# First attention of an eight-layer kernel as a pipeline over sequences, and other slots in its scan

## The chip, the cores and the metric

The kernel runs on one core of a Trainium2 chip. The metric is the device time of one execution in microseconds (us), the median of three runs. The core has five engines with their own in-order queues: TensorE (PE: products and transposes, results in eight PSUM banks), VectorE (DVE), ScalarE (ACT), GpSimd (POOL) and SyncE (SP, which issues DMAs). They meet through semaphores only. All data is float32 unless said otherwise.

## The reference

Eight layers in a row over x of 8 sequences x 512 tokens x 128. Each takes the layer norm of x and adds its answer to x: cosine attention, top-2 experts, feature attention, switch experts, a selective scan, expert-choice experts, attention with relative positions, threshold experts. The change concerns the first layer, the norm and router of the second, and the scan. Cut to these:

```
n = layernorm(x)
Q, K, V = n @ Wq.T + bq, n @ Wk.T + bk, n @ Wv.T + bv          # 128 each
Q = Q / max(norm(Q), 1e-12);  K = K / max(norm(K), 1e-12)
out = softmax(Q @ K.T) @ V                                     # one head, 512 x 512 per sequence
h = relu(out @ W1.T + b1);  h = relu(h @ W2.T + b2)            # 128, 512
x = x + h @ W3.T + b3

n = layernorm(x)
logits = n @ router_w                                          # 8 experts, two are taken per token
...
# selective scan: n -> conv, silu -> xc; (dt, B, C) = projections of xc; 16 states per channel
h[t] = h[t-1] * exp(dt[t] * A) + dt[t] * B[t] * xc[t];   y[t] = sum over states of h[t] * C[t]
y = (y + xc * D) * silu(z);  x = x + y @ W_out
```

## The kernel before

x stays in SBUF as 32 tiles of 128 tokens x 128 (`chip.x`), four tiles a sequence. Every layer is one or more blocks; at the end of a block all engines meet at a barrier (`end_layer` L133, and the end of each `nc.Block`).

`load_stage` (L162) loads x in two transfers of 1 MB, the identity and some tables, turns the relative-position table into a line and waits for all of it. `cosine_attention` (L208) then loads its weights on SP, and the weights of later layers behind them; at L159 SP issues 16 broadcasts of 0.5 MB for the fourth layer (`prepare_later_layers`). Its loop runs twice with four sequences (`W = 4`) per turn. In a turn all four sequences go through one step, then all four through the next; every engine's queue has the steps in this order:

1. VectorE: statistics (L144, L148); ScalarE: square root (L346); VectorE: reciprocal and normalise (L296, L298).
2. TensorE turns the rows (L389), ScalarE copies them out of PSUM (L349), TensorE projects to q, k, v (L396, 384 columns), VectorE adds the bias (L305).
3. Lengths: ScalarE squares (L356), VectorE sums (L310), ScalarE root (L359), VectorE inverts and scales (L313 to L316). TensorE turns q and k (L402), ScalarE copies (L363).
4. Scores (L410), exponential on ScalarE (L367), weighing of v with a column of ones for the denominator (L418), VectorE copies and divides (L324 to L329).
5. Turn o (L425), first layer (L430), second (L435), third (L443); ScalarE does copies and relu (L370 to L377), VectorE adds the bias and then adds to x (L334, L338).

GpSimd prepares tiles for later layers here (`held.prepare`, `features.prepare`) and else does nothing. The function `Banks` (L50) gives each result its PSUM bank by a written list, and with it the waits: a bank is filled only once the last result in it was read.

`top2_glu_experts` (L1044) begins with `normalise_and_route` (L464), a block of its own: statistics and inverse on VectorE and ScalarE, normalise on GpSimd (L532), turned on TensorE (L579), copied (L552), multiplied with the router (L559), with filler products between (`keep_running`, L567); SP stores the normalised rows to memory, from where the experts fetch them. `route` (L596) follows with a copy of the logits out of PSUM (L647) and the softmax and top two on VectorE.

`selective_scan` (L2598) has 128 steps m, 16 states n for each of 8 sequences q. Every engine's queue is written out over m, and what belongs to the next sequences stands in numbered slots n. Per step: SP brings a row of B to all partitions (L2676); GpSimd multiplies it with du (`dBu`, L2731); ScalarE makes the decay in PSUM (`decay`, L2873, two steps ahead); VectorE runs the recurrence (`recur`, L2974, 128x1024) and weighs the state with C (`weigh`, L2983); TensorE spreads C over the partitions (`spread`, L3079, into one bank) and adds up the weighed states (`add_up`, L3096). For states 0, 3 and 6 GpSimd weighs (L2686, from a copy of C by ScalarE, L2779), and `ADDED_AT` says in which slot TensorE adds these. Per sequence TensorE also has `through` (L3086), the step sizes (`step_sizes`, L3067, two halves in one bank), transposes (`turn`, L3037), convolution (L3046), gate (L3053), projection (L3060) and output (`give_out`, L3105). VectorE's `gains(k)` (L2960 to L2967) makes from mean and deviation the factors for normalised rows; `gains(2)` stands right before the first recurrence and serves 24 tiles. ScalarE's `rows_of(q)` (L2759) and `keep_normed(q)` (L2786) use them. `late` is 2 for sequence 0 and 0 for the others.

## Time and profile before

| | |
|---|---|
| median of 3 runs | 3111.35 us (3110.55 to 3114.8) |
| profiled execution | 3111.72 us, its span 3110.0 us |
| mean granted TensorE clock | 0.954 of full |
| TensorE busy | 2814.7 us (91% of the span) |
| VectorE, ScalarE, GpSimd busy | 1643.1, 1511.5, 1591.5 us (53%, 49%, 51%) |
| load stage | 0 to 13.8 us |
| first attention | 13.8 to 212.6 us |
| norm and router of the second layer | 213.7 to 236 us |
| scan | 869 to 1357 us |

The busy time of an engine says how much it had to do, not what set the end; that is read stage by stage from the windows and from the idle time ahead of an instruction (the last bracket of a timeline's row, with the one that ended it). TensorE's clock is given as a share of 2.4 GHz; a window of 0.5 is 1.2 GHz. A float32 product shows as two records, a transpose as one.

### The profile page before, as it was taken

The numbers are of one execution on the slowest core, as the hardware profiler recorded it, in microseconds if no ns is written. First come the engines' busy times: TensorE is split into PE (matmuls) and PEld (weight loads), VectorE is DVE, ScalarE is ACT, GpSimd is POOL, SyncE is SP. The second block draws the span as 40 slices with busy tenths as digits, with TensorE's granted clock in tenths as the row PEclk, the third lists the DMA queues.
The fourth block names the chain that finished last, engine by engine and source line by source line (L and its number), as shares of the span: only waits on it lengthen the run. The fifth ranks groups of instructions, "written<-read, shape, count | busy, mean of one in ns | idle before, by whom it ended". The sixth has DMA issues, their size and how long they took to land. (4 is left out here: it accounts for less than half of the span.)

```text
span 3110.0 us, 44512 instructions
## 1 busy us (share of the span) xinstructions
PE 2814.7 (91%) x14327; PEld 1760.4 (57%) x14354; DVE 1643.1 (53%) x4042; ACT 1511.5 (49%) x3086; POOL 1591.5 (51%) x1622
## 2 busy tenths in 40 slices
PE   6796997896778899767989999999999999999999
PEld 4564996775733344337974444444444444777776
DVE  4436444755368999974335555555555555211112
ACT  3431332332667877622235666666666664433333
POOL 0011775423768999933434555555555554699100
PEclk9898998887999999988989999999999999999999
DMA  5001667101122222243000000000000000000000
GB/s 174 0 24 56 206 206 188 43 1 40 49 82 70 79 75 82 74 122 116 22 12 1 1 0 0 0 0 0 0 0 0 0 1 13 16 8 8 14 7 28
DMA packets 91000, 141.36 MB, mean 45 GB/s; under 512 B 12315, under 2 KB 48038, under 8 KB 90838
## 3 DMA queue, kind: packets, MB, share of 16 engines
q1 hardware_dynamic: 76502, 116.83, 12.1%
q0 software_dynamic: 9728, 19.94, 2.6%
q10 hardware_dynamic: 4608, 2.56, 0.3%
q8 instruction: 86, 1.41, 0.2%
q14 instruction: 76, 0.62, 0.1%
HBM read 122.71 MB, written 24.97 MB: 47 GB/s over the span
## 5 line engine op out<-in xcount | busy, mean ns | idle before, releaser
L1790 POOL TENSOR_TENSOR l3a_p<-l3a_p,l3a_rden 128x512 f32<-128x512 f32 x512 | 521.5, 1040 | 482.2 <-DVE l3a_rden L1826 479.5
L1816 DVE CUSTOM_DVE_ANT_0 l3a_p<-bank,relative_bias 128x512 f32<-128x512 f32 x512 | 333.4, 689 | 211.2 <-PE bank L1965 204.4
L1886 ACT ACTIVATE l3a_p<-l3a_p,l3a_low 128x512 f32<-128x512 f32 x512 | 365.4, 719 | 4.5 <-DVE l3a_low L1816 4.5
L1974 PEld LDWEIGHTS bank<-ident,l3a_p 128*128 128x128 f32 x2048 | 228.5, 141 | 162.5 <-issue 157.9
L2731 POOL TENSOR_TENSOR l2a_dBu<-l2a_du,l2a_bs 128x1024 f32<-128x1024 f32 x128 | 299.1, 2351 | 32.9 <-DVE l2a_h L2974 30.6
L1892 ACT COPY l3a_pT<-bank 128x512 f32<-128x512 f32 x256 | 150.2, 587 | 324.2 <-PE bank L1974 323.8
L2974 DVE TENSOR_TENSOR_SCAN l2a_h<-bank,l2a_dBu 128x1024 f32<-128x1024 f32 x128 | 290.5, 2280 | 9.5 <-ACT bank L2873 8.3
L1559 ACT ACTIVATE l3f_h<-bank,l3f_b 128x512 f32<-128x512 f32 x256 | 175.5, 687 | 244.4 <-PE bank L1667 241.1
L1965 PE MATMUL bank<-l3a_kT,l3a_qT 64*128 64x512 f32 x1024 | 291.3, 645 | 1.2 <-ACT l3a_kT L1877 0.7
L1974 PE MATMUL bank<-ident,l3a_p 128*128 128x128 f32 x2048 | 273.6, 277 | 0.6 <-ACT l3a_pT L1892 0.5
L1676 PEld LDWEIGHTS bank<-l3f_w,l3f_h 128*128 128x128 f32 x2048 | 237.7, 192 | 27.2 <-issue 27.2
L1625 DVE SCALAR_TENSOR_TENSOR x<-bank,l3f_gates,x 128x128 f32<-128x128 f32 x256 | 72.1, 344 | 338.6 <-PE bank L1676 338.4
L1676 PE MATMUL bank<-l3f_w,l3f_h 128*128 128x128 f32 x2048 | 237.9, 275 | 0.0
L1983 PE MATMUL bank<-l3a_pT,l3a_v 128*64 128x512 f32 x1024 | 233.9, 599 | 0.0
L1667 PE MATMUL bank<-l3f_xnT,l3f_w 128*128 128x512 f32 x512 | 232.6, 599 | 0.8 <-ACT l3f_xnT L1550 0.8
L1822 DVE COPY l3a_pT<-bank 128x512 f32<-128x512 f32 x256 | 174.4, 681 | 54.5 <-PE bank L1974 54.3
L3096 PE MATMUL bank<-l2a_hc,ident 128*128 128x512 f32 x416 | 201.4, 608 | 1.9 <-DVE l2a_hc L2983 1.1
L2873 ACT ACTIVATE bank<-l2a_dt,scan_a_neg 128x511 f32<-128x511 f32 x256 | 165.1, 680 | 59.3 <-DVE l2a_h L2974 56.0
L1965 PEld LDWEIGHTS bank<-l3a_kT,l3a_qT 64*128 64x128 f32 x1024 | 78.5, 186 | 161.9 <-issue 157.2
L1019 PE MATMUL bank<-l0fe_xT,l0fe_wi 128*128 128x256 f32 x640 | 147.7, 385 | 1.7 <-issue 1.1
L1667 PEld LDWEIGHTS bank<-l3f_xnT,l3f_w 128*128 128x128 f32 x512 | 93.7, 193 | 95.7 <-issue 95.7
L966 ACT ACTIVATE l0fe_g<-bank,l0fe_wi 128x256 f32<-128x256 f32 x160 | 67.0, 470 | 158.9 <-PE bank L1019 156.0
(523 smaller groups left out, 5008.0 us busy)
## 6 DMA issues: line engine op xcount, KB each, us to landing
l2a_bs<-l2a_b_rows SPq DMA_DIRECT2D x128, 256.0 KB, 3.3
l0fe_wi<-in_L_ffn_in_dram SPq DMA_DIRECT2D x40, 516.0 KB, 4.9
l0fe_wo<-in_L_ffn_out_dram SPq DMA_DIRECT2D x40, 320.0 KB, 3.3
by_place<-by_distance SPq DMA_DIRECT2D x16, 512.0 KB, 14.5
relative_bias<-by_place SPq DMA_DIRECT2D x16, 448.0 KB, 11.5
l3f_w<-in_L_ffn_W_dram SPq DMA_DIRECT2D x16, 256.0 KB, 3.1
switch_out<-in_L_ffn_out_dram SPq DMA_DIRECT2D x1, 2560.0 KB, 19.2
switch_in<-in_L_ffn_in_dram SPq DMA_DIRECT2D x1, 2064.0 KB, 14.4
```

What stands on the lines that cost most here:

```text
L1559: act.activation(h[q][:, j, :], chip.psum[j][:], ACT.Gelu_apprx_tanh, bias=b1[:, e * J + j:e * J + j + 1]).then_inc(hidden_taken, 1)
L1667: pe.matmul(chip.psum[j][:], w1[e % 2][:, j * P:(j + 1) * P], xnT[:, q * S:(q + 1) * S], start=True, stop=True).then_inc(hidden_summed, 1)
L1676: ins = pe.matmul(y_bank[k % 3][:, t * D:(t + 1) * D], h[q][:, j, t * P:(t + 1) * P], w2[e % 2][:, j, :], start=(j == 0), stop=(j == J - 1))
L1790: ins = pool.tensor_tensor(a, a, rden[:, t, h:h + 1].to_broadcast([P, S]), ALU.mult)
L1816: bk.drain(dve.tensor_tensor_reduce(p[u % 2][h][:, t, :], ps(job)[:], bias[:, u % HP * 2 + h, b0:b0 + S], 1.0, 3.0e38, ALU.add, ALU.min, l ...
L1886: ins = act.activation(a, a, ACT.Exp, bias=low[h][:, t:t + 1], scale=-1.0, accum_out=den[:, t, h:h + 1])
L1965: bk.fill(pe.matmul(ps(job)[:], qT[u % 2][half[h], t * P:(t + 1) * P], kT[u % 2][half[h], :], start=True, stop=True), job)
L1974: ins = pe.transpose(ps(job)[:, t * P:(t + 1) * P], p[u % 2][h][:, t, kt * P:(kt + 1) * P], chip.ident[:])
L1983: ins = pe.matmul(ps("av")[half[h], :], v[u // GP % 2][:, kt, c:c + DK3], pT[h][:, kt, :], start=(kt == 0), stop=(kt == TPS - 1))
L2731: pool.tensor_tensor(dBu[m % ND][:], du[q % 2][:], bcast(bs[m % NB][:], n_before=CH), ALU.mult).then_inc(dBu_ready, 1)
L2974: dve.tensor_tensor_scan(h[m % NH][:].rearrange("p c s -> p (c s)"), dA[m % NA].rearrange("p c s -> p (c s)"), dBu[m % ND][:].rearrange("p ...
L3096: ins = pe.matmul(y_bank[j][:], chip.ident[:], weighed[:, j, :], start=False, stop=(m % N == N - 1))
```

## The change

`load_stage` is gone; its loads and the line for the fourth layer are in the attention's block. x comes in eight transfers, one per sequence, each with a semaphore of its own, on SP; weights are issued by ScalarE's queue. The attention is written out for all eight sequences with no loop: in turn i each engine has scores and weighing of sequence i, the MLP of i-1, the norm and router of i-2 on the way out, and transposes and projection of i+2, in an order given step by step for each engine. Inverse roots are powers of -0.5 on GpSimd (`root`, `invert`), which also normalises both ways, adds b3 to x and prepares the later layers' tiles. Outgoing rows are stored as they come; the logits are copied to SBUF and given to `route`, and `normalise_and_route` isn't called for this layer. In the scan the late gains go to GpSimd behind its third product, and `keep_normed`, `rows_of`, the second half of the step sizes and the addition of state 0 have other slots; TensorE has two fillers more in slot 0 of sequences 1 to 7, and one more at the start. The diff, cut to its core:

```diff
+def cosine_attention(chip, a, w, held, w_scan, features, w_features, xn_rows, logits):
...
+        order = [(("line", c), c) for c in range(2)] + [(("xT", 0), 4), (("xT", 1), 5)]
+        order += [(("qkv", q, t), t) for q in range(AHEAD) for t in range(TPS)] + [(("qT", 0), 6), (("kT", 0), 7)]
+        for i in range(B + 2):
+            now, behind, coming, turning, leaving = i < B, 1 <= i <= B, i + AHEAD < B, i + 1 < B, 2 <= i
+            order += [(("s", i, t), t) for t in range(TPS)] if now else []
+            order += [(("oT", i - 1), 6), (("h1", i - 1), 6)] if behind else []
+            order += [(("xT", i + AHEAD), 7)] + [(("qkv", i + AHEAD, t), 7) for t in range(TPS - 1)] if coming else []
+            order += [(("av", i, t), 4 + t % 2) for t in range(TPS)] if now else []
+            order += [(("h2", i - 1, j), j) for j in range(J)] if behind else []
+            order += [(("qT", i + 1), 6), (("kT", i + 1), 7)] if turning else []
+            order += [(("nT", i - 2), 4)] if leaving else []
+            order += [(("y", i - 1), 6)] if behind else []
+            order += [(("logits", i - 2), 5)] if leaving else []
+            order += [(("qkv", i + AHEAD, TPS - 1), 7)] if coming else []
...
+                sp.dma_start(chip.ident[:], a["ident"]).then_inc(ident_loaded, 16)
+                for q in range(B):
+                    sp.dma_start(chip.x[:, cut(q), :], w["x"][q].rearrange("(t p) d -> p t d", p=P)).then_inc(x_loaded[q], 16)
+                sp.dma_start(chip.before[:], a["before"]).then_inc(kept_loaded, 16)
+                sp.dma_start(chip.count[:], a["count"].partition_broadcast(P)).then_inc(kept_loaded, 16)
+                sp.dma_start(chip.token_no[:], a["token_no"]).then_inc(kept_loaded, 16)
                 held.load(sp, w_scan)
                 features.load(sp, w_features)
+                sp.wait_ge(line_stored, 16)
                 prepare_later_layers(chip, sp)
+                sp.wait_ge(zeros_ready, 1)
+                sp.dma_start(xn_rows[0:1, :], chip.zeros[0:1, 0:D]).then_inc(rows_stored, 16)
+                for q in range(B):
+                    sp.wait_ge(left_ready, q + 1)
+                    rows = xn_rows[1 + q * S:1 + (q + 1) * S, :].rearrange("(t p) d -> p t d", p=P)
+                    sp.dma_start(rows, xn_all[:, cut(q), :]).then_inc(rows_stored, 16)
+                sp.wait_ge(kept_loaded, 48)
+                sp.wait_ge(rows_stored, 16 * (B + 1))
...
+                def root(q, n):
+                    pool.wait_ge(mv_ready[n], q + 1)
+                    chip.apart(pool)
+                    c.link(pool.tensor_scalar(var[n][:, cut(q)], mv[n][:, cut(q), 1], LN_EPS, 0.0, ALU.add, ALU.add))
+                    c.link(pool.tensor_tensor(rstd[n][:, cut(q)], var[n][:, cut(q)], minus_half[:].to_broadcast([P, TPS]), ALU.pow))
+
+                def normalise(q, n, out, ready):
+                    chip.apart(pool)
+                    for t in range(TPS):
+                        at = q * TPS + t
+                        ins = pool.tensor_scalar(out[:, t, :], chip.x[:, at, :], minus_mean[n][:, at:at + 1], rstd[n][:, at:at + 1], ALU.add, ALU.mult)
+                    ins.then_inc(ready, 1)
+
+                def come(q):
+                    root(q, "in")
+                    if q >= 2:
+                        bk.wait_filled(pool, ("xT", q - 2), 0)
+                    normalise(q, "in", xn[q % 2], xn_ready)
+
+                def add_bias(q):
+                    pool.wait_ge(xn_ready, q + 1)
+                    pool.tensor_tensor(chip.x[:, cut(q), :], chip.x[:, cut(q), :], bcast(b3[:], n_before=TPS), ALU.add).then_inc(biased, 1)
+
+                def invert(q):
+                    pool.wait_ge(ss_ready, q + 1)
+                    chip.apart(pool)
+                    c.link(pool.tensor_scalar(low[:, q], ss[:, q], 1e-24, 0.0, ALU.max, ALU.add))
+                    pool.tensor_tensor(inv[:, q].rearrange("p t n -> p (t n)"), low[:, q].rearrange("p t n -> p (t n)"),
+                                       minus_half[:].to_broadcast([P, 2 * TPS]), ALU.pow).then_inc(inv_ready, 1)
+
+                pool.wait_ge(half_ready, 1)
+                come(0)
+                come(1)
+                invert(0)
+                come(2)
+                pool.wait_ge(rest_loaded, 16 * 7)
+                for q in range(3):
+                    add_bias(q)
+                for i in range(B + 2):
+                    if i >= 2:
+                        root(i - 2, "out")
+                    if i + 1 < B:
+                        invert(i + 1)
+                    if i >= 2:
+                        normalise(i - 2, "out", xn_all[:, cut(i - 2), :], left_ready)
+                    if i + 3 < B:
+                        come(i + 3)
+                        add_bias(i + 3)
+                    if i == 2:
+                        held.prepare(chip, pool)
+                    if i == 3:
+                        features.prepare(pool)
...
+                come(0)
+                come(1)
+                for k in range(2):
+                    take_line(k)
+                for k in range(2):
+                    bk.wait_read(dve, ("line", k), 0)
+                dve.sem_inc(lined, 1)
+                come(2)
+                dve.wait_ge(qkv_loaded, 16 * 6)
+                for t in range(TPS):
+                    take_qkv(0, t)
+                sum_squares(0)
+                for t in range(TPS):
+                    take_qkv(1, t)
+                scale(0)
+                for i in range(B + 2):
+                    if i >= 2:
+                        add(i - 2)
+                    if i + 1 < B:
+                        sum_squares(i + 1)
+                    if i + AHEAD < B:
+                        take_qkv(i + AHEAD, 0)
+                    if i + 1 < B:
+                        scale(i + 1)
+                    if i < B:
+                        take_weighed(i, 0)
+                        take_weighed(i, 1)
+                    if i + AHEAD < B:
+                        take_qkv(i + AHEAD, 1)
+                    if i < B:
+                        take_weighed(i, 2)
+                    if i + AHEAD < B:
+                        take_qkv(i + AHEAD, 2)
+                    if i < B:
+                        take_weighed(i, 3)
+                    if i + 3 < B:
+                        come(i + 3)
+                    if i < B:
+                        divide(i)
+                    if i + AHEAD < B:
+                        take_qkv(i + AHEAD, 3)
...
+                for q in range(AHEAD):
+                    take_xT(q)
+                square(0)
+                take(("qT", 0), qT[0][:])
+                take(("kT", 0), kT[0][:])
+                act.wait_ge(rest_loaded, 16 * 7)
+                for i in range(B + 2):
+                    if i < B:
+                        exponential(i, 0)
+                        exponential(i, 1)
+                    if i + 1 < B:
+                        square(i + 1)
+                    if 1 <= i <= B:
+                        take(("oT", i - 1), oT[:])
+                    if i < B:
+                        exponential(i, 2)
+                        exponential(i, 3)
+                    if i + AHEAD < B:
+                        take_xT(i + AHEAD)
+                    if 1 <= i <= B:
+                        take_h1(i - 1)
+                        take_h2(i - 1, 0)
+                        take_h2(i - 1, 1)
+                    if i + 1 < B:
+                        take(("qT", i + 1), qT[(i + 1) % 2][:])
+                    if 1 <= i <= B:
+                        take_h2(i - 1, 2)
+                        take_h2(i - 1, 3)
+                    if i >= 2:
+                        take(("nT", i - 2), nT[i % 2][:])
+                    if i + 1 < B:
+                        take(("kT", i + 1), kT[(i + 1) % 2][:])
+                    if i >= 2:
+                        take_logits(i - 2)
...
+                for i in range(B + 2):
+                    if i < B:
+                        scores(i, 0)
+                        scores(i, 1)
+                    if 1 <= i <= B:
+                        turn_o(i - 1)
+                    if i < B:
+                        scores(i, 2)
+                        scores(i, 3)
+                    if i + AHEAD < B:
+                        turn_x(i + AHEAD)
+                    if 1 <= i <= B:
+                        first(i - 1)
+                    if i + AHEAD < B:
+                        project(i + AHEAD, 0)
+                    if i < B:
+                        weigh(i, 0)
+                    if 1 <= i <= B:
+                        second(i - 1, 0)
+                    if i < B:
+                        weigh(i, 1)
+                    if 1 <= i <= B:
+                        second(i - 1, 1)
+                    if i + AHEAD < B:
+                        project(i + AHEAD, 1)
+                    if i + 1 < B:
+                        turn_q(i + 1)
+                    if i < B:
+                        weigh(i, 2)
+                    if 1 <= i <= B:
+                        second(i - 1, 2)
+                    if i + AHEAD < B:
+                        project(i + AHEAD, 2)
+                    if 1 <= i <= B:
+                        second(i - 1, 3)
+                    if i < B:
+                        weigh(i, 3)
+                    if i >= 2:
+                        turn_out(i - 2)
+                    if i + 1 < B:
+                        turn_k(i + 1)
+                    if 1 <= i <= B:
+                        third(i - 1)
+                    if i >= 2:
+                        route_out(i - 2)
+                    if i + AHEAD < B:
+                        project(i + AHEAD, 3)
...
-        SHARED, LATER, ADDED_AT = (0, 3, 6), 4, {0: 5, 3: 12, 6: 13}
+        SHARED, LATER, ADDED_AT = (0, 3, 6), 4, {0: 6, 3: 12, 6: 13}
...
+                def late_gains():
+                    cut = slice(*PARTS[2])
+                    pool.wait_ge(inverted, 1)
+                    c.link(pool.tensor_tensor(shifts[:, :, cut], inv[:, :, cut], bcast(mv[:, cut, 0], n_before=2), ALU.mult))
+                    chip.apart(pool)
+                    pool.tensor_scalar(shifts[:, :, cut], shifts[:, :, cut], -1.0, 0.0, ALU.mult, ALU.add).then_inc(inv_ready, 1)
+                    pool.tensor_scalar(own_gain[:, cut], inv[:, 0, cut], 1.0, 0.0, ALU.add, ALU.add).then_inc(gains_ready, 1)
...
+                    if m == 2:
+                        late_gains()
...
-                    if m in (10, 15):
-                        keep_normed((10, 15).index(m))
+                    if m in (8, 11):
+                        keep_normed((8, 11).index(m))
...
-                        if n == 2:
+                        if n == 2 + late:
                             rows_of(q + 2)
...
-                gains(2)
+                cut = slice(*PARTS[2])
+                dve.wait_ge(std_ready, 3)
+                dve.reciprocal(inv[:, :, cut], std[:, :, cut]).then_inc(inverted, 1)
...
-                keep_running(5, c_bank)
+                keep_running(6, c_bank)
...
+                    if n == 0 and q:
+                        bk.wait_read(pe, ("bc", q + 1) if q + 1 < B else ("z", q - 1, 1), 0)
+                        keep_running(2, chip.psum[7])
                     if n == 1:
                         through(q)
+                    if n == 3 + late and q + 1 < B:
+                        step_sizes(q + 1, 1)
                     if m in dve_no:
                         add_up(m)
                     if m in pool_adds:
                         add_up(pool_adds[m])
-                    if n in (1 + late, 2 + late) and q + 1 < B:
-                        step_sizes(q + 1, n - 1 - late)
+                    if n == 1 + late and q + 1 < B:
+                        step_sizes(q + 1, 0)
...
-        load_stage(chip, a["L0_attn_x"], a["ident"], a["before"], a["count"], a["token_no"],
-                   a["L3_attn_rel_bias"], a["L3_attn_onehot"])
-        chip.end_layer()
```

## Rows read from the trace of the kernel before

**Rows 1.** Page, part 1: busy us (share of span) xinstructions.

```profile
PE 2814.7 (91%) x14327; PEld 1760.4 (57%) x14354; DVE 1643.1 (53%) x4042; ACT 1511.5 (49%) x3086; POOL 1591.5 (51%) x1622
```

**Rows 2.** Windows: length, busy PE, PEld, DVE, ACT, POOL; clock, DMA share, GB/s.

```profile
0.00:14.00 14.00, 3.59 (x4) 0.41 (x4) 1.75 (x8) 0.00 (x1) 0.19 (x4) 1.00 0.66 181
14.00:50.00 36.00, 18.68 (x74) 13.72 (x75) 29.35 (x91) 13.20 (x23) 6.26 (x10) 0.91 0.82 261
50.00:114.00 64.00, 62.32 (x352) 44.70 (x350) 14.45 (x48) 28.78 (x44) 0.00 (x0) 1.00 0.08 26
114.00:150.00 36.00, 21.39 (x82) 14.71 (x83) 29.18 (x88) 12.86 (x24) 0.00 (x0) 0.76 0.00 0
0.00:237.00 237.00, 187.72 (x970) 131.53 (x970) 101.46 (x363) 90.00 (x152) 20.30 (x46) 0.95 0.22 66
```

**Rows 3.** Timeline of TensorE: start us, us, instruction, count [idle before, releaser].

```profile
24.04 3.67 PE L389 MATMUL bank<-ident,l0a_rows 128*128 128x128 f32 x16 [16.58 <-DMA l0a_b<-in_L_attn_b_dram]
27.51 10.53 PE L396 MATMUL bank<-l0a_w_qkv,l0a_turned 128*128 128x384 f32 x32
44.84 4.46 PE L402 MATMUL bank<-ident,l0a_h 128*128 128x128 f32 x24 [6.80 <-DVE l0a_h L316]
...
50.70 13.90 PE L410 MATMUL bank<-l0a_qT,l0a_kT 128*128 128x512 f32 x32
64.44 14.46 PE L418 MATMUL bank<-l0a_qkv,l0a_E 128*128 128x129 f32 x128
78.73 2.27 PE L425 MATMUL bank<-ident,l0a_rows 128*128 128x128 f32 x16
80.84 3.60 PE L430 MATMUL bank<-l0a_turned,l0a_w 128*128 128x512 f32 x8
```

**Rows 4.** Timeline where the norm stage ends and route begins.

```profile
231.39 1.74 POOL L532 TENSOR_SCALAR l0f_xn_all<-x,l0fr_rstd,l0fr_shift 128x128 f32<-128x128 f32 x4 [0.45 <-DVE l0fr_shift L523]
...
234.08 2.00 PE L559 MATMUL bank<-l0fr_router,l0fr_xnT 128*128 128x8 f32 x16
...
236.52 0.42 DVE L647 COPY l0fg_logits<-bank 128x256 f32<-128x256 f32 x1 [5.34 <-PEq L484]
```

**Rows 5.** GpSimd in later layers: the power by line, an addition by group.

```profile
L1514 POOL TENSOR_TENSOR l3f_rstd<-l3f_var,l3f_minus_half x8: 1028/1028/1031, 2639.4 to 2662.2; 128x4 f32<-128x4 f32 x8
...
L1790 POOL TENSOR_TENSOR l3a_p<-l3a_p,l3a_rden 128x512 f32<-128x512 f32 x512 | 521.5, 1040 | 482.2 <-DVE l3a_rden L1826 479.5
```

**Rows 6.** Window in the steady part of the scan, columns as above.

```profile
1075.00:1130.00 55.00, 50.11 (x131) 21.88 (x134) 52.00 (x33) 43.44 (x67) 51.30 (x24) 0.97 0.27 78
```

**Rows 7.** Groups of VectorE, 906 to 1346: busy us, mean ns | idle before.

```profile
L2983 DVE TENSOR_TENSOR l2a_hc<-l2a_h,bank 128x1024 f32<-128x1024 f32 x102 | 122.3, 1199 | 20.8 <-PE bank L3079 12.1 <-remote 8.7
```

**Rows 8.** Timeline of VectorE in the scan, rows with idle time ahead.

```profile
922.27 2.29 DVE L2974 TENSOR_TENSOR_SCAN l2a_h<-bank,l2a_dBu 128x1024 f32<-128x1024 f32 x1 [2.88 <-ACT bank L2873]
...
965.07 2.29 DVE L2974 TENSOR_TENSOR_SCAN l2a_h<-bank,l2a_dBu 128x1024 f32<-128x1024 f32 x1 [1.46 <-ACT bank L2873]
969.37 2.29 DVE L2974 TENSOR_TENSOR_SCAN l2a_h<-bank,l2a_dBu 128x1024 f32<-128x1024 f32 x1 [2.01 <-ACT bank L2873]
985.38 1.22 DVE L2983 TENSOR_TENSOR l2a_hc<-l2a_h,bank 128x1024 f32<-128x1024 f32 x1 [3.72 <-PE bank L3079]
...
1041.37 1.22 DVE L2983 TENSOR_TENSOR l2a_hc<-l2a_h,bank 128x1024 f32<-128x1024 f32 x1 [2.38 <-remote]
...
1096.07 1.22 DVE L2983 TENSOR_TENSOR l2a_hc<-l2a_h,bank 128x1024 f32<-128x1024 f32 x1 [2.29 <-PE bank L3079]
```

**Rows 9.** Gains by line: duration ns min/median/max, first and last start.

```profile
L2965 DVE SCALAR_TENSOR_TENSOR l2a_shifts<-l2a_mv,l2a_inv x3: 161/376/2145, 876.0 to 901.6; 128x4 f32<-128x4 f32 x2, 128x24 f32<-128x24 f32 x1
...
L2967 DVE TENSOR_SCALAR l2a_own_gain<-l2a_inv x3: 160/163/2319, 876.1 to 903.8; 128x4 f32<-128x4 f32 x2, 128x24 f32<-128x24 f32 x1
```

**Rows 10.** Windows of 2 us at a turn of the scan, columns as above.

```profile
1028.00:1030.00 2.00, 0.00 (x0) 0.00 (x0) 2.00 (x2) 1.71 (x3) 2.00 (x2) 1.00 0.25 55
...
1032.00:1034.00 2.00, 2.00 (x3) 0.67 (x2) 2.00 (x2) 1.38 (x4) 2.00 (x2) 0.50 0.02 7
```

477 lines of the change are left out of this document (227 added, 250 removed).

## The prediction, made before the changed kernel ran

> **What bounds the kernel now.** I read the page's totals first: TensorE is busy 91% of the span [rows 1], so the question is what stands in the missing 9% and what changes hands where. Then the windows by stage, for the first 237 us, all of which the change rewrites [rows 2]. The reader is to see two kinds of stretch. In 50 to 114 us TensorE is busy 62.3 of 64 us. In 0 to 14, 14 to 50 and 114 to 150 us it is busy 3.6, 18.7 and 21.4 us, and there VectorE has 29 of 36 us: four sequences go through each step together, so at the two heads of the loop TensorE stands before the norm, the projection's evictions and the lengths. The row of the whole stretch gives VectorE 101.5 and ScalarE 90.0 us over 8 sequences, 12.7 and 11.3 each; neither can be what paces a stage in which TensorE needs more than that. Third, TensorE's timeline, for the price of each step and the waits before it: idle 16.6 us ahead of the first transposes and 6.8 us ahead of the turned q and k [rows 3]. Last the end of the norm stage [rows 4]: last normalise over at 233.13, route's copy of the logits at 236.52, its first own operation at 236.98.
>
> In the scan VectorE is the pace: 52.0 of 55 us, GpSimd 51.3, TensorE 50.1 [rows 6]. VectorE's idle time in 906 to 1346 us is, above all, 20.8 us ahead of the weighing [rows 7], and the timeline shows where it lies, at the turns from one sequence to the next [rows 8].
>
> The sums are made against the profiled execution: 3111.72 us, of which the span is 3110.0 and 1.7 lie around it. It is 0.4 us above the median of 3111.35, which I neglect.
>
> **First attention: what TensorE has to do.** From rows 3, start to start, per sequence: a transpose 0.132 us (16 in 2.11), 20 of them (x, q, k, o, and the outgoing rows) 2.64; the four projections 2.63 (16 in 10.53); scores 3.44 (16 products in 13.74, each two records); weighing 16 products at 0.223 (64 in 14.29), 3.57; first layer one such product as the scores have four, 0.86; second layer as many and as wide as the scores, 3.44; third layer as many as the weighing, 3.57; router 0.96, taken as the norm stage has it (16 records in 2.00 for two sequences, rows 4). Sum 21.1 us, 169 us for eight. All this work is done before too; the filler products of the norm stage go.
>
> **The other engines beside it.** VectorE loses the normalise of the way in, the second addition of y and the 32 small copies of denominators, and gains nothing but a 4-element negation per norm: about 10.7 of its 12.7 us. ScalarE loses the square roots and all changes of function table but one: about 10 us. GpSimd is new: per sequence two norms of four instructions at 0.44 (1.74 each, the row of rows 4), three powers and the small operation ahead of each, and the bias. The trace has the power on 128x4 at 1.03 us [rows 5]; the one on 128x8 isn't in it, I bound it by 1.0 and 2.1 and take 1.6. Bias 1.04, as the nearest addition of 128x512. Together 3.5 + 1.0 + 2 x 1.3 + 1.9 = 9 us. None reaches 21.1, so TensorE paces the loop, if no queue puts a wait before it. I walked through one turn in the written order. Waits that I find: the projection after the turned x stands 0.3 us behind ScalarE's copy (which has two exponentials, the squares and oT ahead of it), and turned o stands close to VectorE's addition of y, which has the last projection's eviction ahead of it. I take 0.6 us a turn, 4 us in all; bounds 0 and 2.5 a turn. GpSimd's preparation for later layers (6.3 us, the busy time of rows 2 in 14 to 50, once) has a turn with 12 us of slack in which to hide.
>
> **Head.** x comes in eight transfers and the weights on ScalarE's queue at the same time, instead of 14 us of loading and then the weights. Per transfer 0.25 MB; at the 261 GB/s of rows 2 one takes 1 us and I take the first landed at 4.3. From there a chain of single steps: statistics 1.6, power 1.3 and normalise 1.7 on GpSimd, twice since x of two sequences is turned before the first projection, turned 12.8, copied 13.4; four projections with evictions to 16.1, squares 1.1, sum 1.2, evictions of sequence 1 to 20.7 (the inverse length hides under them), scaling 1.3, q and k turned and copied 1.8: scores start at 24 us. Before they start at 50.7. TensorE has done 7.4 us of its 169 by then.
>
> **Tail.** The pipeline empties over two turns: 24 + (169 - 7.4 - 1.5 of the last sequence's outgoing part) + 4 + 2.4 (copies of oT and h1 with nothing to put between) = 190.5 us for the last y. Then addition and statistics 2.3, power 1.4, normalise 1.75, and from there to the next stage 3.6 (3.3 in rows 4; the two small operations on A's rates, which were hidden, now stand behind the last logits; route's copy of the logits is gone). That is 199.5. TensorE stands idle for 5 us twice in the head and once in the tail, and runs at half clock after such gaps (0.76 of full clock in 114 to 150, rows 2): 3 us for that. Route's first own operation at 202.5 against 236.98: **34.5 us less**. Bounds: 44 with no bubbles and no cold clock, 16 with 2.5 us a turn.
>
> **Rows and stores.** SP now stores the normalised rows one sequence at a time, the last behind the last normalise as before: hidden as before. The sixteen broadcasts of 0.5 MB start at 12 instead of 25 us and are needed only in the fourth layer; the weights for the pipeline are ahead of them. Cost nothing; if they delayed the weights of the MLP, these have until 24 us.
>
> **The scan.** Three places. (1) The start. The gains of 24 tiles: two of VectorE's small operations on 128x24 took 2145 and 2319 ns beside GpSimd's first long products, where the 128x4 forms take 161 and 160 [rows 9]. They held back the first recurrence, at 906.0. Now VectorE has the reciprocal only and the first recurrence can start when the first dBu is there, 903.7: 2.3 us. GpSimd gets four small operations behind its third product, some 1.2 us, and it has 3.7 us of idle time in the 55 of rows 6. ScalarE's rows of sequence 2 (1.65 us) stood before a decay for which VectorE waited 2.88 [rows 8]; moved two slots on, 1.6 more. I take 3.4 for both. (2) The turn from sequence 0 to 1: two batches of keep_normed (1.6 us each) stood together at step 15, and the waits of 1.46 and 2.01 follow [rows 8]. At steps 8 and 11 they stand apart: 2.5. (3) Each later turn: TensorE idles 2.2 us after the first spread, is at half clock in 1032 to 1034 [rows 10], and then its second dt product waits for ScalarE before the spread that VectorE needs: 3.72, 2.38 and 2.29 at the first three [rows 8], then 2.24, 2.22 and 3.90, 16.8 us over six turns, with two of 0.98 behind, 18.7. The two fillers (1.7 us) lie in the gap and the dt product goes behind the spread. The period of a turn is 54.7 us (1041.37 to 1096.07, rows 8); scaled to it, rows 6 give GpSimd 51.0 us of work and VectorE 51.7, so GpSimd takes over soon. I take not 18.7 but 10. Sum of the scan **16 us**; bounds 0 (the new pace is TensorE, below) and 24.
>
> 3111.7 - 34.5 - 16 = **3061**.
>
> **Rivals.**
> A. The written order doesn't hold: waits of 2.5 us a turn and a head 4 us later; the attention gives 16 instead of 34.5. For it: every queue is in order and h1, h2, oT have one buffer. Against: 62.3 of 64 us in rows 2 with the same engines. 3080.
> B. The scan gives nothing: TensorE has 49.8 us in a turn of 54.7 (rows 6, scaled), less 1.9 at half clock and with 1.7 of fillers about 49.6 in a turn of 52, and stands in the way itself, or GpSimd does. 3111.7 - 34.5 = 3077, and 3089 if the seven pairs of fillers (12 us) come on top.
> C. All better: no bubbles, scan 24: 3111.7 - 44 - 24 = 3044.
> D. Slower. Mechanism: VectorE and GpSimd stop one another. In rows 9 a small VectorE operation took as long as the GpSimd one beside it. With all of it in turn, 10.7 + 9 = 19.7 us a sequence, still below 21.1; slower only if TensorE also stands at each handover: to lose what head, tail and scan give (some 57 us from 3061 to 3118) takes 7 us a turn over eight turns, a turn of 28.8 us. With a dozen handovers, 0.6 us at each. It would stand in the windows as VectorE and TensorE both under 75%.
> The Trainium skill (SBUF — State Buffer, section "SBUF: two separate sides") calls the pair shared by VectorE and GpSimd an exclusive lock held for a whole instruction. By that rule D's premise holds for every scaling and division here, not only for rows 9; the sum of 19.7 already grants it, so it gives D its mechanism and leaves D's chance small.
> E. The new load order starves the head: weights land late behind x. 24 us becomes 34, the former place of x; 3071. Inside the range.
>
> **How the numbers follow.** Forecast 0.57 (E with it), A 0.12, B 0.14, C 0.12, D 0.05. Likeliest 3061; its own range 3050 to 3072. For 8 in 10: from 3045 (most of C) to 3085 (A and most of B). A measurement here tells 0.2%, 6 us: faster 0.94, same 0.02, slower 0.04.
>
> **What would show it.** Scores of sequence 0 start near 24; scores of successive sequences 21 to 22 us apart; route's first reduction near 202; VectorE's wait of 2.2 to 3.9 in the weighing gone at each turn and the period there 52 to 53.5 instead of 54.7; the first recurrence 2.3 us after the product's start as against 4.6; the through products at 0.43 a record. Wrong, if the scores are over 24 us apart (A), if the scan's period stays above 54 (B), or if the shift after 237 us is not what is left at the end.

## The result, and where the time went

Four runs of each on one chip: before 3111.97 us (3110.55 to 3114.8), after 3092.55 us (3087.73 to 3096.72), ratio 0.9934 with a 95% interval of 0.9918 to 0.995. Faster, as forecast, but by 19.4 us instead of 50, and outside the range of 3045 to 3085. The profiled run took 3091.65 us, its span 3089.9.

I followed the same operations through both traces and noted by how much each starts earlier after the change:

| place | before | after | earlier by |
|---|---|---|---|
| first scores of the first attention | 50.70 | 28.77 | 21.9 |
| route's first operation | 236.98 | 206.27 | 30.7 |
| first recurrence of the scan | 906.0 | 873.0 | 33.0 |
| first operation behind the scan | 1358.2 | 1311.7 | 46.5 |
| fourth layer's attention, answer of sequence 0 added | 1769.5 | 1722.4 | 47.1 |
| the same, sequence 6 | 2519.8 | 2500.1 | 19.7 |
| end of the span | 3110.0 | 3089.9 | 20.1 |

So both parts of the change gave nearly what they were to give, 47 us by 1722 us, and an attention that the change does not touch lost 27 of them again. It does so in six nearly equal steps: its loop turns every 125.0 us before and every 129.3 to 129.8 us after.

The page after, part 1 (to be read beside [rows 1]) and the queue of instructions in part 3. VectorE and ScalarE have less to do, GpSimd 68 us more, TensorE the same.

```profile
PE 2817.8 (91%) x14334; PEld 1755.5 (57%) x14362; DVE 1620.1 (52%) x3942; ACT 1499.5 (49%) x3065; POOL 1659.3 (54%) x1713
...
q14 instruction: 107, 0.88, 0.1%
```

The windows of the new first attention, columns as in [rows 2]: head, pipeline, and the way out to route.

```profile
0.00:28.80 28.80, 14.24 (x37) 7.17 (x37) 12.35 (x47) 4.69 (x6) 11.93 (x25) 0.93 0.93 278
28.80:195.20 166.40, 160.43 (x895) 113.31 (x895) 66.87 (x209) 71.15 (x120) 73.24 (x104) 0.99 0.15 45
195.20:206.40 11.20, 3.72 (x19) 3.13 (x18) 2.21 (x11) 1.32 (x5) 3.00 (x6) 0.66 0.08 23
```

In the middle TensorE is busy 160.4 of 166.4 us, and no other engine half the time. That is what the whole of [rows 2] lacked at its two heads.

TensorE's timeline at both ends, to be read beside [rows 3] and [rows 4]:

```profile
5.46 3.59 PE L592 MATMUL bank<-l0a_onehot,l0a_table 32*16 32x512 f32 x4 [5.46 <-DMA l0a_onehot<-in_L_attn_onehot_dram]
11.11 1.09 PE L509 MATMUL bank<-ident,l0a_xn 128*128 128x128 f32 x4 [2.06 <-issue]
14.33 1.12 PE L509 MATMUL bank<-ident,l0a_xn 128*128 128x128 f32 x4 [2.13 <-POOL l0a_xn L258]
15.24 6.67 PE L520 MATMUL bank<-l0a_w_qkv,l0a_xnT 128*128 128x384 f32 x16
25.93 1.97 PE L509 MATMUL bank<-ident,l0a_qk 128*128 128x128 f32 x8 [4.03 <-DVE l0a_qk L337]
28.77 3.78 PE L535 MATMUL bank<-l0a_qT,l0a_kT 128*128 128x512 f32 x5 [0.87 <-ACT l0a_kT L414]
...
191.33 3.81 PE L571 MATMUL bank<-l0a_w,l0a_h 128*128 128x128 f32 x32 [0.54 <-ACT l0a_h L446]
...
200.93 1.12 PE L509 MATMUL bank<-ident,l0a_xn_all 128*128 128x128 f32 x4 [5.00 <-POOL l0a_xn_all L258]
202.72 1.87 PE L584 MATMUL bank<-l0a_router,l0a_nT 128*128 128x8 f32 x8 [0.67 <-ACT l0a_nT L414]
```

Now the loss. VectorE's timeline at the end of the first turn of the fourth layer's loop, after the change. L2033 is the turn's last operation, L2020 the first of the next:

```profile
1722.36 0.69 DVE L2033 TENSOR_TENSOR x<-bank,x 128x512 f32 x1 [1.06 <-PE bank L2197]
1727.66 0.69 DVE L2020 COPY l3a_pT<-bank 128x512 f32<-128x512 f32 x1 [4.61 <-issue]
```

"Issue" means that the profile shows nothing that VectorE waited for: its operands were there. VectorE's groups in 1720 to 2480 us give the sum of it, 28.2 us, which is near the 27 that were lost (what a wait really costs is read on TensorE further down). In the window from 1720 to 1850 us, one turn, the only transfers are of instructions, five of 8 KB:

```profile
L2020 DVE COPY l3a_pT<-bank 128x512 f32<-128x512 f32 x188 | 128.1, 681 | 66.3 <-PE bank L2172 38.0 <-issue 28.2
```

```profile
q14 instruction: 5, 0.04, 0.1%
```

Three of the five come right after the branch back, at 1723.5, 1725.9 and 1728.4 us, two later, at 1777.3 and 1826.6. Counting all of VectorE's records, register operations and branches included, a turn has 323, and the loop starts at record 2878. In its first turn there are fetches where VectorE is at records 2881, 3011 and 3138, some 128 apart. (Two more, at 3025 and 3030, are taken for those of other engines: the 107 transfers of q14 are more than VectorE's 5741 records would fill.) The theory from this (P, place of the code): what matters is where the loop lies against the pieces of 8 KB. On three pieces it stays held and is not fetched again while it runs; on four (here two or three records, 128, 128 and the rest) its beginning has been overwritten when the branch comes back, and VectorE stands until it is there. The loop itself is unchanged; VectorE's program ahead of it has become 27 instructions shorter, by the written ones.

### The profile page after: what moved, and what is told of

Its sections match the earlier page's. It is cut to its first block and busy times, and to the rows that moved or that the text cites. A ratio compares the mean times of both kernels' runs of the same rounds, so it can differ in the third digit from the quotient of the medians.

```text
span 3089.9 us, 44369 instructions
## 1 busy us (share of the span) xinstructions
PE 2817.8 (91%) x14334; PEld 1755.5 (57%) x14362; DVE 1620.1 (52%) x3942; ACT 1499.5 (49%) x3065; POOL 1659.3 (54%) x1713
## 3 DMA queue, kind: packets, MB, share of 16 engines
q8 instruction: 89, 1.46, 0.2%
## 5 line engine op out<-in xcount | busy, mean ns | idle before, releaser
L3183 DVE TENSOR_TENSOR_SCAN l2a_h<-bank,l2a_dBu 128x1024 f32<-128x1024 f32 x128 | 290.8, 2280 | 13.8 <-POOL l2a_dBu L2938 7.8
L1874 PEld LDWEIGHTS bank<-l3f_w,l3f_h 128*128 128x128 f32 x2048 | 237.6, 192 | 27.3 <-issue 27.3
L2020 DVE COPY l3a_pT<-bank 128x512 f32<-128x512 f32 x256 | 174.4, 681 | 82.4 <-PE bank L2172 54.2
L3082 ACT ACTIVATE bank<-l2a_dt,scan_a_neg 128x511 f32<-128x511 f32 x256 | 165.1, 680 | 53.5 <-DVE l2a_h L3183 49.9
L2135 PE MATMUL bank<-relative_xnT_all,relative_w_qk 128*128 (+1 forms) x256 | 139.6, 628 | 8.1 <-ACT l3a_qT L2073 5.0
```

The source lines that it names most:

```text
L1874: ins = pe.matmul(y_bank[k % 3][:, t * D:(t + 1) * D], h[q][:, j, t * P:(t + 1) * P], w2[e % 2][:, j, :], start=(j == 0), stop=(j == J - 1))
L3183: dve.tensor_tensor_scan(h[m % NH][:].rearrange("p c s -> p (c s)"), dA[m % NA].rearrange("p c s -> p (c s)"), dBu[m % ND][:].rearrange("p ...
```

## The experiments

The first four ran on a chip on which the kernel before took 3111.33 us, the other eight on slower ones (3168.59 and 3167.63); each ratio is to runs of the kernel before on the same chip. What is read from a stage is read from the trace.

**The loop put back where it was.**

```
+                for _ in range(27):
+                    chip.apart(dve)
                 for t in range(TPS):
                     least(0, 0, t)
```

> The changed kernel with 27 increments of a semaphore that nobody waits for, on VectorE at the start of the fourth layer's attention, ahead of its loop. Nothing in the loop is touched. By the trace of the changed kernel the loop of 323 records starts 3 records ahead of a place where the next 8 KB of instructions is fetched, and fetches come 128 records apart, so its body lies on four such pieces; before it started 26 behind such a place and lay on three. The 27 put it back to where it was before. Theory P (place of the code): the 4.6 us ahead of each turn's first copy and the five 8 KB fetches a turn are gone, 27 us less, 3065 us. Rival R1 (the stall comes from something else that the change moved, the clock, data transfers or a phase between the engines): unchanged, 3092, perhaps 1 us more for the 27 instructions.

3066.98 us, ratio 0.9848 [0.9813, 0.9882]. The turns take 125.0 us. The same place of VectorE's timeline, the same group in 1720 to 2480 us, and the queue in the page:

```profile
1728.94 0.69 DVE L2033 TENSOR_TENSOR x<-bank,x 128x512 f32 x1 [1.06 <-PE bank L2199]
1729.87 0.69 DVE L2020 COPY l3a_pT<-bank 128x512 f32<-128x512 f32 x1 [0.24 <-PE bank L2174]
```

```profile
L2020 DVE COPY l3a_pT<-bank 128x512 f32<-128x512 f32 x193 | 131.5, 681 | 40.6 <-PE bank L2174 40.6
```

```profile
q14 instruction: 77, 0.63, 0.1%
```

Thirty transfers fewer, five for each of six turns, and no "issue" left. R1, a cause other than the place, is out: 27 instructions that do nothing made the kernel 25 us faster.

**The same done to the kernel before.** The same two lines with 101.

> The kernel before with 101 such increments at the same place, nothing else changed: its loop then starts 127 records behind the last fetching place, 1 ahead of the next, so that its body lies on four pieces as that of the changed kernel does. Theory P: it gets the same stall, six times 4.3 to 4.7 us, 3111 + 27 and at most some 2 for the 101 instructions = 3138 to 3141 us. Rival R1: 3111 to 3114.

3114.63 us, ratio 1.0013 [0.9997, 1.0029]. A miss in size: the five fetches a turn are there (107 in the page), the loss is 0.7 us a turn, not 4.6.

```profile
1769.60 0.69 DVE L1835 TENSOR_TENSOR x<-bank,x 128x512 f32 x1 [1.06 <-PE bank L2001]
1772.64 0.69 DVE L1822 COPY l3a_pT<-bank 128x512 f32<-128x512 f32 x1 [2.35 <-issue]
```

The first copy waits for one load. Six records later there is a second wait, of 1.28 us, and both are mostly made up in the turn, where VectorE has idle time. In the changed kernel one record stands between the two waits, and the first copy waits for both. So the fetches alone don't set the price; how many records of the loop the first piece holds does. How, the mirror below shows. My count of the shift was five off as well: by these two traces the change moves the loop by 22 places, not 27.

**The two parts one by one.** The new attention with the old scan, and the new scan in the kernel before; no line besides.

> The new first attention with norm and router inside, and the scan as it was before. VectorE's program has 24 instructions less ahead of the fourth layer's loop than before, so the loop starts 2 records behind a fetching place: three pieces. Theory P: the attention's 30.7 us in full, 3081 us, no fetch in the loop. Rival R2 (the new attention brings the loss with it, through what it leaves behind for the later layers): 3108.

> The kernel before with the scan's new slots alone. Three VectorE instructions less ahead of the fourth layer's loop: 23 behind a fetching place, three pieces. The traces give the scan 16.2 to 16.6 us: 3095.5 us. If the scan's gain hangs on how the attention before it leaves the engines: 3100 or more. If the scan brings the loss in the fourth layer: 3122.

3082.11 us, 0.9902 [0.987, 0.9934], and 3099.38 us, 0.9962 [0.9949, 0.9975]: 29.2 and 12.0 us. Both have turns of 125.0 us in the fourth layer. 41.2 in sum, against 44.4 with both and the loop in its place: the parts add up within what these runs tell, and neither brings the loss. Only together do they shift the code far enough (24 and 3 written instructions: the loop's first record goes from place 21 of its piece to place 2, and then over the edge to the last place of the piece before). R2 is out.

**One instruction.** If one record of the loop lies in the first piece, one instruction ahead of it is enough (`range(1)`).

> The changed kernel with a single increment of a semaphore that nobody waits for, on VectorE ahead of the fourth layer's loop. In the trace of the changed kernel the stall has two parts: 2.84 us from the branch back to the loop's first record and 2.35 us from it to the second, the first copy. Of the run of the kernel before with 101 instructions more, six records come between its first and its second stall. So in the changed kernel the piece of 8 KB in which the loop begins holds one record of it. Theory P2: with one instruction more the loop begins with a piece, lies on three, and stays held: no fetch in it, turns of 125.0 us instead of 129.6, 27 us less than the changed kernel, 3065 us. Rival R3 (it takes a shift of some size, the position to the instruction doesn't matter): still 3092.

3122.38 us where before has 3168.59: ratio 0.9865 [0.9834, 0.9897]; all six turns 125.0 us, 77 transfers. It hangs on the single instruction, and R3 (a shift of some size is needed) is out.

**The mirror.** The kernel before with 106 instead of 101.

> The kernel before with 106 instructions more ahead of the same loop instead of 101. By the count of records in the run with 101 (six in the first piece) the first piece now holds one record, as in the changed kernel. Theory P2: turns of 129.6 us instead of 125.7 with 101 and 125.0 before: 3111 + 27 = 3138 us. Rival R4 (the large stall belongs to the changed kernel alone, and before can only get the small one): 3115.

3192.53 us, ratio 1.0083 [1.0059, 1.0106], 24 us slower. Turns of 128.0 and then 129.5 to 129.9 us.

```profile
1823.41 0.69 DVE L1835 TENSOR_TENSOR x<-bank,x 128x512 f32 x1 [1.06 <-PE bank L2001]
1828.77 0.69 DVE L1822 COPY l3a_pT<-bank 128x512 f32<-128x512 f32 x1 [4.67 <-issue]
```

Five instructions between a loss of 5 us and one of 26 over the six turns, in a kernel that has nothing of the change. R4 (only the changed kernel can have the large loss) is out.

Why the second load costs so much more stands on TensorE, which waits for that first copy. It stood 2.61 us in the changed kernel and 0.42 us with `range(101)`:

```profile
1728.41 1.11 PE L2172 MATMUL bank<-ident,l3a_p 128*128 128x128 f32 x4 [2.61 <-DVE l3a_pT L2020]
```

```profile
1773.39 0.66 PE L1976 MATMUL bank<-ident,l3a_p 128*128 128x128 f32 x4 [0.42 <-DVE l3a_pT L1822]
```

And behind the longer wait its granted clock fell to the lower level. Windows, columns as in [rows 2], of the changed kernel, then of the mirror after its first branch back and after its second:

```profile
1728.20:1731.20 3.00, 2.79 (x8) 1.29 (x8) 2.05 (x7) 1.52 (x4) 1.47 (x2) 0.50 0.01 3
```

```profile
1829.50:1832.90 3.40, 3.39 (x18) 1.85 (x18) 2.47 (x9) 2.18 (x6) 2.04 (x2) 1.00 0.01 2
1958.30:1961.50 3.20, 3.20 (x7) 0.56 (x5) 0.94 (x4) 1.80 (x5) 2.04 (x2) 0.50 0.00 0
```

In the changed kernel the clock falls in each of the six turns. In the mirror it does not in the first, which takes 128.0 us, and does in the five others, which take 129.5 to 129.9; TensorE stood 2.74 and 2.62 us there. With one load it never falls. So of the 4.6 us a turn some 3 are the wait itself, and some 1.6 the lower clock behind it.

**Four pieces, cut elsewhere.** The changed kernel with `range(72)`.

> The changed kernel with 72 instructions more ahead of the loop: the loop begins with the last 57 places of a piece, lies on four pieces, and the fourth holds 10 of its records. Theory P2: five fetches of 8 KB a turn as in the changed kernel, but only one load stands ahead of the first copy (2.4 us) and the second piece comes while the first runs: turns of 125.5 to 126.5 us, 3 to 9 us more than with the loop on three pieces, 3068 to 3074 us. If four pieces cost the same whatever the split: 3092.

3125.53 us, 0.9871 [0.9847, 0.9895]; turns of 125.6 to 125.9 us, 4 us over the six. The wait ahead of the first copy is 2.42 us, one load, and the turn makes most of it up:

```profile
1781.54 0.69 DVE L2020 COPY l3a_pT<-bank 128x512 f32<-128x512 f32 x1 [2.42 <-issue]
```

All the traces together: counted from the kernel with one instruction, whose loop begins with a piece, the first record lies at place 0, 2, 3, 18, 21 or 26 in the kernels with turns of 125.0 to 125.1 us, at place 71 or 122 in the two with small losses, and at place 127 in the two with large ones. The first group has no transfer in its turns but, in some, one within 0.5 us of the last branch; the others have five in each.

**The head, loads.** Scores started 4.8 us later than forecast. The seven loads of the later weights go from ScalarE's queue to SP's, behind x:

```
-                act.dma_start(w1[:], w["W1"]).then_inc(rest_loaded, 16)
+                sp.dma_start(w1[:], w["W1"]).then_inc(rest_loaded, 16)
...
```

> The changed kernel with the one instruction of the run above, and the seven loads of the later weights (W1, W2, W3, b3, b1, b2, router) issued by SP behind x instead of by ScalarE. In the trace of the changed kernel ScalarE issues transfers until 12.6 us, loads its function table until 13.9 and only then takes the first turned x, which was there at 12.2; scores started at 28.77 where 24 was forecast. Theory H: the first copy of the turned x comes at 12.3 instead of 13.96 and scores start 1.6 us earlier, 27.2; the time 1.6 us below that of the run with one instruction. Rival H2 (TensorE's half clock and the first projection's weights set the start anyway): scores at 28.8, no change. Rival H3: the later weights land late behind x and the 0.9 MB for the scan, scores start after 29.

3126.47 us, 0.9867 [0.984, 0.9895], no change. ScalarE's first copy came at 12.16 instead of 14.43; scores at 29.85. Theory H falls, H2 holds in part: the projections stood behind the second turning of x, which waited for GpSimd. H3's sign, scores after 29, is there, but it was already with the one instruction alone (29.20), and the first projection started at 15.16 against 15.11: nothing shows a wait for the later weights.

```profile
14.25 1.12 PE L509 MATMUL bank<-ident,l0a_xn 128*128 128x128 f32 x4 [2.13 <-POOL l0a_xn L266]
15.16 7.82 PE L520 MATMUL bank<-l0a_w_qkv,l0a_xnT 128*128 128x384 f32 x16
```

**The head, order.** On top of it:

```
                 for q in range(AHEAD):
                     turn_x(q)
-                pe.wait_ge(qkv_loaded, 16 * 6)
-                for q in range(AHEAD):
+                    pe.wait_ge(qkv_loaded, 16 * 6)
                     for t in range(TPS):
                         project(q, t)
```

> The changed kernel with one instruction more, the later weights issued by SP, and TensorE's first steps in the order x of sequence 0 turned, its four projections, x of sequence 1 turned, its four projections (both were turned first). With the loads moved alone the first copy came at 12.16 instead of 14.43 and nothing moved, as the second turning stood ahead of the projections and waited for GpSimd's norm until 14.25. Theory H4 (the order on TensorE's queue sets the start): first projection at 12.9 instead of 15.1, scores at 27.3 instead of 29.2, 1.5 to 2 us less than the kernel with one instruction more. Rival: the square of sequence 0 stands behind the copy of sequence 1 on ScalarE and eats it, scores at 29.

```profile
12.51 5.40 PE L520 MATMUL bank<-l0a_w_qkv,l0a_xnT 128*128 128x384 f32 x8 [0.78 <-DMA l0a_b_qkv<-in_L_attn_bv_dram]
...
19.07 2.82 PE L520 MATMUL bank<-l0a_w_qkv,l0a_xnT 128*128 128x384 f32 x8 [0.72 <-issue]
...
27.61 5.52 PE L535 MATMUL bank<-l0a_qT,l0a_kT 128*128 128x512 f32 x8 [0.87 <-ACT l0a_kT L422]
```

Scores at 27.61 against 29.20 with one instruction alone, 1.6 us. But the nine traces with the new attention and the old order have anything from 28.77 to 30.72, and part of that is TensorE's pace. Two of them reached full pace when this one did (17.7 to 17.9 us), and their scores start at 28.77 and 28.83: by these the order is worth 1.2 us. So H4 holds in sign and is a little smaller than its 1.5 to 2. In the time, 3120.11 us and 0.9859 [0.9838, 0.9881], it can't be told from 0.9865. The two halves of the projections are the same work: 5.40 us and 2.82 us.

TensorE's pace explains it. The step from one projection record to the next is 0.64 us at first and 0.32 us later. In twelve of the fourteen traces the one step between the two lengths is also where the trace's records of the granted clock begin, at 17.94 us in the changed kernel and 20.18 with the loads moved. In the other two, this one (17.68) and the scan alone, they begin where no projection runs. Ahead of that place there is no record of the clock, and a window's row shows 1.00 for want of one; the two rows at the end of this document are to be read so. What lifts the pace there, no run here tells.

**The scan, part by part,** each on top of the one instruction. The old turn:

```
-                    if n == 0 and q:
-                        ...
-                        keep_running(2, chip.psum[7])
...
-                    if n == 3 + late and q + 1 < B:
-                        step_sizes(q + 1, 1)
...
+                    if n in (1 + late, 2 + late) and q + 1 < B:
+                        step_sizes(q + 1, n - 1 - late)
```

> The changed kernel with one instruction more on VectorE (loop of the fourth layer on three pieces), and in the scan the turn as it was: no two fillers, both step-size products ahead of the through products again. The prediction gave this part 10 of the scan's 16 us. From first to last recurrence: before 438.9, 438.0 and 439.3 us in the traces with the old slots, 425.4 to 427.9 in those with the new. If the prediction's split holds, this kernel stands at 436 to 437 there, and 10 us above the kernel with one instruction more. Rival: the gain lies in the first turn's keep_normed, and this one stands at 429 to 432.

The last gains on VectorE again (`gains(2)` for the reciprocal, `late_gains` gone):

> The changed kernel with one instruction more, and the last gains on VectorE ahead of the first recurrence as before. From the first dBu product to the first recurrence: 4.6 us as before instead of 2.45; the rest of the scan unchanged, so 2 us above the kernel with one instruction more. If GpSimd's four small operations cost it as much where they stand, the time is the same.

And `m in (10, 15)` for `m in (8, 11)`:

> The changed kernel with one instruction more, and keep_normed of the first turn at steps 10 and 15 instead of 8 and 11. The prediction gave this 2.5 us: recurrences over 429 instead of 426.7 us, the turn from sequence 0 to 1 longer, all others the same. Rival: with the other slots changed it is hidden, 426.7.

| scan with | first dBu to first recurrence | first to last recurrence | from sequence to sequence |
|---|---|---|---|
| all old (four traces) | 4.65 | 435.6 to 439.3 | 54.0, 61.2, 54.8, 54.7, 54.7, 54.6, 56.8 (before) |
| all new (seven traces) | 2.45 | 425.4 to 427.9 | 55.0, 55.2, 54.4, 54.4, 54.4, 53.2, 51.7 (one instruction) |
| old turn | 2.46 | 435.9 | 55.1, 57.1, 57.5, 54.9, 54.7, 54.7, 53.7 |
| old gains | 4.65 | 427.1 | 55.3, 54.0, 54.4, 54.4, 54.4, 54.4, 51.8 |
| old keep | 2.45 | 428.0 | 53.8, 59.1, 54.4, 53.2, 53.2, 54.4, 51.8 |

Times 3129.09, 3126.19 and 3129.15 us, ratios 0.9881 [0.9854, 0.9907], 0.9885 [0.9859, 0.9912] and 0.9886 [0.9865, 0.9908]. The intervals overlap that of the new scan, so the sizes are those of the stage. The turn is worth 9 us (435.9 against 426.6), the gains 2.2, keep_normed 2.7 over the first two turns. Over the whole scan keep_normed shows 1.4, less than the 2.5 by which the seven traces of the new scan differ among themselves. Not tried alone: the slots of `rows_of` and of the addition of state 0, the one filler more at the start, and, inside the turn, the fillers without the later step sizes. VectorE's timeline with the gains back shows the two operations at the length of [rows 9], the groups below it what the turn does to the wait of [rows 7]: the scan with the old turn first, then the changed kernel, each from its first to its last recurrence.

```profile
923.85 2.15 DVE L3165 SCALAR_TENSOR_TENSOR l2a_shifts<-l2a_mv,l2a_inv 128x24 f32<-128x24 f32 x1
...
926.01 2.32 DVE L3167 TENSOR_SCALAR l2a_own_gain<-l2a_inv 128x24 f32<-128x24 f32 x1
```

```profile
L3194 DVE TENSOR_TENSOR l2a_hc<-l2a_h,bank 128x1024 f32<-128x1024 f32 x103 | 123.5, 1199 | 16.4 <-PE bank L3292 16.4
L3206 DVE TENSOR_TENSOR x<-bank,x 128x512 f32<-128x512 f32 x7 | 4.7, 673 | 0.7 <-PE bank L3318 0.7
```

```profile
L3192 DVE TENSOR_TENSOR l2a_hc<-l2a_h,bank 128x1024 f32<-128x1024 f32 x103 | 123.2, 1196 | 1.1 <-PE bank L3290 1.1
L3204 DVE TENSOR_TENSOR x<-bank,x 128x512 f32<-128x512 f32 x7 | 4.8, 683 | 4.4 <-PE bank L3316 4.4
```

15.3 us of wait are gone ahead of the weighing; 3.7 come back ahead of the addition of the answers, and those ahead of the recurrences, 13.8 us in the changed kernel, were there with the old turn too (12.9).

What the new turn does to TensorE shows in its through products, before and after, each over the recurrences:

```profile
L3086 PE MATMUL bank<-l2a_xc,scan_d_diag 128*128 128x512 f32 x32 | 26.5, 978 | 5.6 <-DVE l2a_sz L2989 5.6
```

```profile
L3297 PE MATMUL bank<-l2a_xc,scan_d_diag 128*128 128x512 f32 x32 | 17.5, 673 | 5.6 <-DVE l2a_sz L3198 5.6
```

From start to start a record takes 0.85 us before in six of the eight sequences, and 0.43 after in seven; with the old turn put back, 0.85 again in five. The clock also sorts the new turns. From the third to the sixth, in the nine traces that have them, seven take 53.2 us and twenty-nine 54.3 to 54.4. The granted clock stays at 1.00 through each of the seven and falls in each of the twenty-nine. One of either kind in the changed kernel:

```profile
983.22:1036.42 53.20, 50.13 (x134) 21.82 (x136) 51.87 (x32) 42.93 (x67) 50.67 (x24) 1.00 0.25 80
1089.62:1144.02 54.40, 51.70 (x134) 22.47 (x137) 51.87 (x32) 42.94 (x67) 51.09 (x24) 0.97 0.28 79
```

## Why the prediction was wrong

The failed step is the one that had no term: "3111.7 - 34.5 - 16 = 3061" takes every layer behind the change as it was. "If the shift after 237 us is not what is left at the end" stood among the things that would show it wrong, and the fourth layer's loop shows it: 27.3 us given back. What the sum had at nothing is VectorE's program behind the change: moved by 22 places, the loop lay on four pieces of code instead of three, VectorE waited for two of them after each branch back, 4.6 us a turn, and TensorE with it. With the loop in its place the kernel takes 3067 us, inside the range and 6 over the forecast. None of the rivals had this. Part of it could have been seen: VectorE's count of instructions ahead of a loop is known from the diff, and a trace of before shows fetches of 8 KB and none between the loop's branches. That four pieces are not held, and what that costs, the trace of before does not show.

The Trainium skill (Runtime: NRT & Kernel Launch, section "Instruction fetch mechanics") has the rule that was missing: "A taken branch whose target isn't in the current 2-page window forces a DMA fetch of the target page before execution can continue". The traces agree with the mechanism and add the price here, 2.4 us a load ahead of the first copy. They differ on the size for VectorE: that section of the Trainium skill has blocks of 16 KB, two of them held; the transfers of its program are of 8 KB and 128 records apart, and the same 323 records are held on three such pieces and not on four. By the 512 instructions that it says are held, the loop might have been thought safe. Two blocks of 16 KB fit the runs at no alignment. The changed kernel's loop is fetched anew and stays held with one instruction more, so it would have to begin one place ahead of a block. With 72 more it would then lie on two blocks and be held, and yet its trace has five transfers a turn.

The steps:

- **TensorE paces the attention, 21.1 us a sequence.** Right. The pipeline from the first scores to the last y (195.14) took 166.4 us; 190.5 - 24 = 166.5 was forecast. From sequence 2 on scores start 21.0, 22.1, 21.0 and 21.0 us apart. GpSimd's 73.2 us over it are 9.2 a sequence, 9 forecast; the power on 128x8 took 1.66, taken at 1.6. Rivals A (turns over 24 us) and D (VectorE and TensorE both under 75%) are out. D's premise was right all the same. GpSimd's normalising operations take 0.44 to 0.46 us each, and the five of them that lie beside VectorE's scaling of q and k take 1.48 to 1.49: they waited for it, as D assumed. It cost nothing, with GpSimd busy 44% of the time.
- **Slips in the sums.** The router's 16 records in 2.00 us for two sequences are 1.00 each, not 0.96, 0.3 us in all. Rival A's terms, 2.5 us a turn over eight turns in place of 4 in all and a head 4 us later, take 20 us from 34.5 and leave 14.5, not 16. Neither changes the forecast.
- **Head, 24 us.** 28.77, in three terms. The first projection started at 15.24 where the turned x was to be copied by 13.4: 1.8. ScalarE issued sixteen transfers until 12.7 and loaded its table until 13.9, but by the run that moves seven of them this costs nothing by itself; the order of the two turnings costs 1.2 to 1.6 us. From there to the last eviction of sequence 0 (19.9; 16.1 forecast) 4.7 us instead of 2.7: the first projection records took 0.85 us each instead of 0.49, at half the later pace, as the experiment on the order shows. From there to the scores 8.9 instead of 7.9: q and k were turned at a granted clock of 0.50, the lower level of 1.2 GHz, after TensorE had stood for 4.03 us. The 3 us for a slow TensorE I had put into the tail's sum. Window after, columns as in [rows 2]:

```profile
25.80:28.00 2.20, 1.97 (x8) 1.57 (x8) 0.08 (x1) 0.65 (x2) 1.96 (x4) 0.50 1.01 302
```

- **Tail.** Last y to route 11.1 us, 12 forecast with those 3 in it. -34.5 + 4.8 - 0.1 - 0.9 gives the -30.7 of the first table.
- **Rows and stores, no cost.** Nothing shows one. E didn't happen: the later weights were there when scores began.
- **Scan, 16 us.** 16.2 for the whole block in the first pair of traces, 13.3 as the mean of four old and seven new (11.1 over the recurrences, 2.2 ahead), 12.0 in the time of the scan alone. The first pair has the shortest of the seven new (425.4 of 425.4 to 427.9) and one of the longer old, so that 16 was met there is in part luck. Start: 2.2 of 3.4. The 1.6 for ScalarE's rows did not come: the wait of 2.88 is gone, but four waits of 1.2 to 1.6 us for GpSimd's product stand in sequence 0. Turn 0 to 1: 2.7 over the two turns it touches, of 2.5. Later turns: 9 of 10, but not as I had it. The wait at each turn is gone as forecast. The period there is 53.2, inside the forecast of 52 to 53.5, only where TensorE keeps its full clock, and 54.4 in most turns; part of what is saved is taken up by the addition of the answers. From the old turn to the new, in the two traces with one instruction more, the seven turns gain 0.1, 1.9, 3.1, 0.5, 0.3, 1.5 and 2.0 us. B is out as a whole, though its sign, a period above 54, was there in most turns: I had named a sign that does not tell B from a gain elsewhere.
- **Through products at 0.43 a record.** Seen, in seven of the eight sequences, against 0.85 before.

What stays open: why the granted clock falls in some turns of the scan and not in others of the same code, and why it stayed up in the mirror's first turn, where TensorE stood no less long.

## What to carry to other kernels

A change moves the code of every loop behind it. Compare the transfers on the queues of instructions before and after; where idle time stands as "issue" behind a loop's branch, shift the loop by a few instructions, or check how many pieces it lies on, before looking for a cause in the data. Look at the granted clock behind every wait of TensorE: here a third of the price lay behind the wait and not in it. Follow the same operation through both traces layer by layer: it takes one table to see that a gain was made and where it was given back. And a wait that goes is not a period that shrinks by as much; read what is late next in the same turn.
